# Four chunks to a PSUM bank in the table products of an edge pass, and 320 of 832 pairs by them instead of 416

## The chip, the cores and the metric

One core of a Trainium2 chip runs the whole program. The metric is the device time of one execution in microseconds, shown as the median of three runs; the profile comes from a further execution. A difference under about 0.2% can't be told from none.

## The reference

Four graph layers over the same 200000 edges (`src`, `dst`, sorted by `dst`) and 6250 nodes of 128 features. What the change touches is the edge part of the last layer:

```python
h = jnp.maximum(_layernorm(x, axis=-1), 0.0)
h = jnp.concatenate([h[row], edge_attr], axis=1)
h = jax.nn.relu(h @ W1a + b1a) @ W1b + b1b
sums = jax.ops.segment_sum(h, col, num_segments=n_nodes)
```

The kernel splits the first product: `h @ W1a[:128]` is made once per node (the "table"), `edge_attr @ W1a[128:] + b1a` once per edge (the "edge rows", stored in DRAM as `bucketed`). Per edge it remains to add the table row of its source to its edge row, to take the positive part, and to sum over the edges of each target node; `W1b` comes after the sum. So the rows of the table have to be fetched 200000 times by index.

## The kernel before

Edges are ordered into 49 x 49 = 2401 buckets (target tile of 128 nodes, source tile of 128 nodes), then cut into chunks of 128 edges; two chunks make a pair, and all edges of a pair go to one target tile. There are 832 pairs, 1664 chunks. Two ways lead from an index to a table row:

- **By gather** (the second 416 pairs, `FAR_PAIRS`). GpSimd issues one indirect DMA a chunk (L1841) into `ring`, SyncE loads the pair's edge rows (L1852), VectorE adds them (`message`, L1954), rectifies (`rectify`, L1959), builds the one-hot matrix of the targets (L1947), TensorE multiplies (L1937), VectorE adds the result to the target tile `h` (`add`, L1965). Rings: `ring` and `edge_in` have DEEP = 8 pairs, one-hots four.
- **By products with the table in SBUF** (the first 416 pairs, 832 chunks, `NEAR`). A chunk needs one look-up for each source tile that its edges touch: VectorE compares the chunk's sources, broadcast to all partitions in `rows`, with the numbers of a tile (`looks`, L1979) into one of eight `hot` slots, and TensorE multiplies that one-hot by the table's tile (`look_up`, L1920) and adds it into the chunk's PSUM bank. ScalarE has first copied the chunk's edge rows into that bank (`prepare`, L1873) and afterwards takes the positive part out of it (`evict`, L1880) and stores it to `near_rows` in DRAM, four chunks in one transfer (L1904). A chunk has a whole bank, of which it uses 128 of 512 columns, and there are four banks, 4 to 7.

Which tile and which chunk a look-up belongs to are known only at run time. The lists `chunk_of` and `tile_of` have LOOKS = 3248 entries; TensorE and VectorE each read eight entries of both lists into registers for a pair (L1926, L1928; L1969, L1971) and compute addresses from them. ScalarE reads four ends (L1896): the count of look-ups after which a chunk is whole. LOOKS is the largest count that could occur (832 + 2401 + 2, rounded up); entries behind the real ones point at a dump chunk, number `NEAR`, and are worked off the same way. Waits: a one-hot waits that its chunk's bank is prepared (`s_clear`) and that the look-up seven before it is done (`s_looked`); the look-up waits for the one-hot.

Both ways run side by side in the first block ("block A"). The order on each engine is written out by hand: in pair `n` VectorE does `message(n)`, eight one-hots, `rectify(n)`, `add(n-1)`, the target one-hots of `n+3`; TensorE does eight look-ups and then the product of gathered pair `n`. 416 x 8 places are enough for 3248 entries, so the last ten pairs have no look-ups. The second block ("block B") then reads `near_rows` back in quads of four chunks (L2014, a ring of eight quads) and sums them into the target tiles: one-hots L2036, products L2027, adds L2044.

Of the kernel before, what the change touches and what calls it, by code (L numbers as in the profile page):

```python
# [4 lines left out]
P = 128  # L5
# [51 lines left out]
PER_PAIR = 8  # L57
QUAD = 4
EPS = 1e-5
SLOPE = 0.2  # L60
assert NEAR % (4 * QUAD) == 0 and FAR_PAIRS * PER_PAIR >= LOOKS and LOOKS % PER_PAIR == 0 and MARKS < DUMP
# [55 lines left out]
def build(nc, t, out):  # L117
    ctx = ExitStack()
    with ctx:
# [1021 lines left out]
        def near_tables():  # L1141
# [29 lines left out]
            def vector(e):  # L1171
# [11 lines left out]
                e.scalar_tensor_tensor(chunk_of, low_i.bitcast(i32), float(16 - EARLY), look_no[:, :], ALU.add, ALU.add).then_inc(code.sem, 1)  # L1183
# [3 lines left out]
                e.tensor_scalar(chunk_of.bitcast(i32), chunk_of, float(NEAR + 16), None, op0=ALU.min).then_inc(listed.sem, 1)  # L1187
# [607 lines left out]
        def edge_pass():  # L1795
# [10 lines left out]
            stage = slots(QUAD * P, 2)  # L1806
            tile_of = room(LOOKS).bitcast(i32)[0:1, :]
            chunk_of = part(wide, 0, LOOKS).bitcast(i32)[0:1, :]
            rows = part(wide, LOOKS, 16 * P // 2).bitcast(i16)
            near_edge = part(wide, LOOKS + 16 * P // 2, 3 * QUAD * P).rearrange("p (k w) -> p k w", k=3)  # L1810
            end_of = src_i[0:1, 0:NEAR]
            s_got = [sem(f"meta_got{k}") for k in range(DEEP)]
            s_side = [sem(f"meta_side{k}") for k in range(DEEP)]
# [5 lines left out]
            s_near_edge = [sem(f"near_edge{k}") for k in range(3)]  # L1819
            row_in = [Baton(s_piece[k], 4 * sage_loads) for k in range(4)]  # L1820
# [8 lines left out]
            def bank(c):  # L1829
                return psum[:, 4 + c % 4, 0:P]  # L1830

            with nc.Block() as block:
                @block.gpsimd
                def _(e):
                    for n in range(FAR_PAIRS):
                        k = n % DEEP
                        if n >= DEEP:
                            e.wait_ge(s_pe, n - DEEP + 1)
                        for c in range(PAIR):
                            chunk = (NEAR_PAIRS + n) * PAIR + c  # L1840
                            e.indirect_dma_start(ring[:, k, c, :], None, table,  # L1841
                                                 bass.IndirectOffsetOnAxis(ap=src_i[:, chunk:chunk + 1], axis=0)).then_inc(s_got[k], 16)

                @block.sync
                def _(e):
                    e.dma_start(chunk_of, look_chunk[:, 0:LOOKS]).then_inc(lists.sem, 16)
                    e.dma_start(tile_of, look_tile[:, 0:LOOKS]).then_inc(lists.sem, 16)
                    for n in range(FAR_PAIRS):
                        k = n % DEEP
                        if n >= DEEP:  # L1850
                            e.wait_ge(s_sum, n - DEEP + 1)
                        e.dma_start(edge_in[:, k, :, :], bucketed_v[:, cols(NEAR_PAIRS + n), 0:D]).then_inc(s_side[k], 16)  # L1852

                @block.scalar
                def _(e):
                    def load_edges(g):
                        e.dma_start(near_edge[:, g % 3, :].rearrange("p (c w) -> p c w", c=QUAD),
                                    bucketed_v[:, g * QUAD:(g + 1) * QUAD, 0:D]).then_inc(s_near_edge[g % 3], 16)

                    def load_rows(g):  # L1860
                        at = g % 4 * QUAD * P
                        e.dma_start(rows[:, at:at + QUAD * P], near_src[g * QUAD:(g + 1) * QUAD, :].rearrange("c n -> (c n)").unsqueeze(0)
                                    .broadcast_to([P, QUAD * P])).then_inc(row_in[g % 4].sem, 16)

                    def prepare(c):
                        g = c // QUAD
                        if c == NEAR:
                            e.copy(bank(c), zeros[:, 0:P]).then_inc(s_clear, 1)
                            return
                        if c % QUAD == 0:  # L1870
                            e.wait_ge(s_near_edge[g % 3], 16 * (g // 3) + 16)
                            e.wait_ge(row_in[g % 4].sem, row_in[g % 4].at + 16 * (g // 4) + 16)
                        e.copy(bank(c), near_edge[:, g % 3, c % QUAD * P:(c % QUAD + 1) * P]).then_inc(s_clear, 1)  # L1873

                    def evict(c, end):
                        g = c // QUAD
# [4 lines left out]
                        e.wait_ge(staged.sem, staged.at + c + 1)  # L1881

                    e.sem_inc(s_clear, 15)
                    e.dma_start(end_of, chunk_end[:, 0:NEAR]).then_inc(s_near_out[0], 16)
                    for g in range(3):
                        load_edges(g)
                    for g in range(4):
                        load_rows(g)
                    e.wait_ge(blanked.sem, blanked.at + 4)
                    for c in range(4):  # L1890
                        prepare(c)
                    e.wait_ge(s_clear, 15 + QUAD)
                    load_edges(3)
                    e.wait_ge(s_near_out[0], 16)
                    for g in range(quads):
                        _, end = nc.values_load_multi_w_load_instructions(  # L1896
                            end_of[0:1, g * QUAD:(g + 1) * QUAD], engines=(ENG.Activation,), min_val=1, max_val=LOOKS,
                            skip_runtime_bounds_check_because=reason)
                        for k in range(QUAD):
                            c = g * QUAD + k  # L1900
                            evict(c, end[k])
                            if c + 4 <= NEAR:
                                prepare(c + 4)
                        e.dma_start(near_rows[:, g * QUAD * D:(g + 1) * QUAD * D], stage[:, g % 2, :]).then_inc(s_near_out[g % 2], 16)  # L1904
                        if g + 4 < quads:
                            e.wait_ge(s_clear, 15 + QUAD * (g + 2))
                            load_edges(g + 4)
                            load_rows(g + 4)
# [4 lines left out]
                def _(e):  # L1913
                    for k in range(4):
                        e.matmul(psum[:, 4 + k, 0:P], lhsT=blank[:, 0:P], rhs=blank[:, 0:P], start=True, stop=True).then_inc(blanked.sem, 1)
                    e.wait_ge(lists.sem, lists.at + 32)

                    def look_up(i, chunk, tile):
                        e.wait_ge(look.sem, look.at + i + 1)
                        e.matmul(flat[:, ds((chunk & 3) * 512 + 2048, P)], lhsT=hot[:, i % 8, :], rhs=table_in[:, ds(tile * P, P)],  # L1920
                                 start=False, stop=True, skip_group_check=True).then_inc(s_looked, 1)

                    for n in range(FAR_PAIRS):
                        if n * PER_PAIR < LOOKS:
                            here = slice(n * PER_PAIR, (n + 1) * PER_PAIR)
                            _, chunk = nc.values_load_multi_w_load_instructions(  # L1926
                                chunk_of[0:1, here], engines=(ENG.PE,), min_val=16, max_val=NEAR + 16, skip_runtime_bounds_check_because=reason)
# [178 lines left out]
```

## Time and profile before

| | us |
|---|---|
| median of 3 runs | 9367.44 (9365.83 to 9368.25) |
| the profiled execution | 9366.17 |
| its span | 9364.4 |
| TensorE busy | 7028.5 (75%) |
| VectorE busy | 5660.6 (60%) |
| GpSimd busy | 2656.2 (28%) |
| ScalarE busy | 2515.7 (27%) |
| mean granted clock of TensorE | 0.87 |

Busy time leaves out what an engine's sequencer does by itself: computing addresses, waiting, and reading numbers into registers (TENSOR_LOAD). Such instructions are found under their line, with the engine's name and a q (`PEldq`, `DVEq`). A matmul of float32 leaves two records, so that `x16` in a timeline are eight look-ups. The granted clock is a share of TensorE's full 2.4 GHz; 0.50 is the level of 1.2 GHz.

### The profile page before, as it was taken

What the parts mean: (1) busy time and instruction counts of PE and PEld (TensorE: products, weight loads), DVE (VectorE), ACT (ScalarE), POOL (GpSimd) and SP (SyncE); (2) the same over time, 40 slices, a digit from 0 to 9 for tenths busy, and PEclk for the clock granted to TensorE, in tenths of its full rate; (3) what the DMA queues carried; (4) which work ended last, traced back from release to release, by engine and by line L of the source; (5) the groups of instructions that cost most, each with busy time, mean ns of one, the idle gap of its engine ahead of it and who ended that gap; (6) DMA issues with size and microseconds to landing.
All of it is one profiled execution on the core that took longest, in us unless ns stands there. A gap on an engine that the chain in (4) does not pass through costs nothing. (4 is left out here: it accounts for less than half of the span.)

```text
span 9364.4 us, 133857 instructions
## 1 busy us (share of the span) xinstructions
PE 7028.5 (75%) x35740; PEld 4596.9 (49%) x35792; DVE 5660.6 (60%) x16783; ACT 2515.7 (27%) x5863; POOL 2656.2 (28%) x2952
## 2 busy tenths in 40 slices
PE   4777777775566659940488699999998777777787
PEld 4555555453122224420477544444445666666676
DVE  6777777775589990059899800000014777777786
ACT  0222222222467740020388600000001333310001
POOL 0777777776470000000000000000002444444410
PEclk9767776766679989975799899999999999999998
DMA  3333333334975538849566478787886766642363
GB/s 99 103 103 105 105 104 103 105 105 167 393 231 164 168 114 306 299 195 426 205 215 216 144 262 276 262 287 256 295 284 200 181 180 179 179 111 63 63 178 88
DMA packets 969628, 1759.77 MB, mean 188 GB/s; under 512 B 102288, under 2 KB 665125, under 8 KB 905315
## 3 DMA queue, kind: packets, MB, share of 16 engines
q1 hardware_dynamic: 683820, 1335.73, 44.1%
q0 software_dynamic: 110720, 276.01, 9.0%
q10 hardware_dynamic: 174394, 139.51, 5.5%
q8 instruction: 346, 5.67, 0.3%
q14 instruction: 348, 2.84, 0.1%
HBM read 1412.04 MB, written 338.80 MB: 187 GB/s over the span
## 5 line engine op out<-in xcount | busy, mean ns | idle before, releaser
L768 POOL DMA_INDIRECT bucketed<-arena,wide x1563 | 1515.6, 970 | 726.5 <-issue 714.0
L1920 PE MATMUL psum<-wide,arena 128*128 x6496 | 1209.9, 329 | 400.5 <-DVE arena L1979 393.9
L1920 PEld LDWEIGHTS psum<-wide,arena 128*128 128x128 f32 x6496 | 989.9, 195 | 618.3 <-issue 493.3
L1787 POOL DMA_DIRECT2D table<-wide x13 | 9.7, 743 | 4316.2 <-DVE wide L1711 4316.2
L1979 DVE TENSOR_SCALAR arena<-wide,tile_first 128x128 f32 x3248 | 870.8, 300 | 472.3 <-PE psum L1920 293.8
L1841 POOL DMA_INDIRECT arena<-table,src_i x832 | 803.3, 966 | 1009.1 <-PE psum L1937 872.4
L1660 PE MATMUL psum<-arena,h 128*128 128x512 f32 (+1 forms) x2548 | 1048.6, 570 | 19.1 <-DMA arena<-adjacency 17.5
L922 PE MATMUL psum<-arena 128*128 128x512 bf16 x2253 | 695.7, 442 | 435.0 <-DVE arena L870 259.4
L665 PE MATMUL psum<-arena 128*113 128x177 bf16 x1568 | 534.4, 341 | 416.2 <-ACT wide L687 374.6
L870 DVE TENSOR_SCALAR arena<-sums 128x512 bf16<-128x512 int16 x2304 | 799.9, 347 | 0.0
L659 PE MATMUL psum<-w_edge,arena 128*128 128x256 f32 x1568 | 786.9, 597 | 0.0
L1660 PEld LDWEIGHTS psum<-arena,h 128*128 128x128 f32 x2548 | 470.0, 191 | 573.7 <-issue 552.6
L1546 PE MATMUL psum<-sums,arena 128*128 128x129 f32 x4802 | 602.2, 281 | 154.1 <-DVE arena L1536 154.1
L922 PEld LDWEIGHTS psum<-arena 128*128 128x128 bf16 x2304 | 240.5, 104 | 883.5 <-issue 722.3
L869 DVE TENSOR_SCALAR arena<-sums 128x128 bf16<-128x128 int16 x2304 | 582.7, 253 | 127.5 <-PE psum L922 126.5
L1546 PEld LDWEIGHTS psum<-sums,arena 128*128 128x128 f32 x4802 | 555.8, 192 | 200.6 <-DVE arena L1536 200.5
L687 ACT CAST wide<-psum 49x49 f16<-49x49 f32 x1568 | 311.6, 199 | 973.9 <-PE psum L665 750.7
L665 PEld LDWEIGHTS psum<-arena 128*113 128x113 bf16 x1568 | 262.9, 168 | 624.5 <-ACT wide L687 623.6
L603 PE MATMUL psum<-blank 128*128 128x120 bf16 x3296 | 531.9, 261 | 18.6 <-PEq L101 18.6
L1660 PE MATMUL psum<-arena,sums 128*128 128x512 f32 (+1 forms) x1274 | 524.1, 571 | 9.3 <-DMA arena<-adjacency 8.6
L1220 PE MATMUL psum<-arena,h 128*128 128x512 f32 (+1 forms) x1274 | 518.5, 570 | 8.8 <-DMA arena<-adjacency 8.6
L1734 DVE TENSOR_TENSOR arena<-psum,wide 128x512 f32<-128x512 f32 (+1 forms) x39 | 25.5, 659 | 786.5 <-PE psum L1660 784.2
(398 smaller groups left out, 11006.0 us busy)
## 6 DMA issues: line engine op xcount, KB each, us to landing
arena<-adjacency SPq DMA_DIRECT2D x294, 1024.0 KB
arena<-adjacency SPq DMA_DIRECT2D x98, 1568.0 KB, 7.8
adjacency<-wide SPq DMA_DIRECT2D x588, 256.0 KB
arena<-adjacency SPq DMA_DIRECT2D x196, 640.0 KB, 3.9
arena<-adjacency SPq DMA_DIRECT2D x147, 768.0 KB
arena<-bucketed POOLq DMA_DIRECT2D x208, 528.0 KB, 6.0
arena<-adjacency SPq DMA_DIRECT2D x49, 1792.0 KB, 6.9
arena<-adjacency SPq DMA_DIRECT2D x49, 1344.0 KB, 6.1
```

The lines of the kernel that those rows point to most:

```text
L603: e.matmul(spare, lhsT=blank[:, 0:P], rhs=blank[:, 0:spare.shape[1]], start=first, stop=True, skip_group_check=True)
L659: e.matmul(terms(k, c), lhsT=attr[k][:, at:at + P], rhs=W["edge"][:, :, :].rearrange("p c n -> p (c n)"), start=True, stop=True)
L665: update = e.matmul(psum[0:SPAN, 0, 0:TILES + P], lhsT=hot[k][:, c, by_dst], rhs=hot[k][:, c, by_both], start=False, stop=True, skip_group ...
L768: e.indirect_dma_start(bucketed, bass.IndirectOffsetOnAxis(ap=places[k][0:size, c:c + 1], axis=0), rows[k][0:size, c, :], None).then_inc(s ...
L869: e.tensor_scalar(hot_src[:, k, :], from_one[:, 0:P], row_of[:, ds(i * RUN + k, 1)], None, op0=ALU.is_equal)
L870: e.tensor_scalar(hot_key[:, k, :], from_one[:, 0:GROUP * P], key_of[:, ds(i * RUN + k, 1)], None, op0=ALU.is_equal).then_inc(s_ready, 1)
L922: e.matmul(flat[:, ds((bucket[k] & (BANKS - 1)) * 512, 512)], lhsT=hot_src[:, k, :], rhs=hot_key[:, k, :], start=False, stop=True, skip_gr ...
L1546: last = e.matmul(psum[:, 4 * (r % 2) + c // 3, 129 * (c % 3):129 * (c % 3) + 129], lhsT=slots[n % 4][:, c * P:(c + 1) * P], rhs=node_rhs( ...
L1660: last = e.matmul(psum[:, 4 * (p % 2) + j, 0:width], lhsT=nodes[:, q * P:(q + 1) * P], rhs=pieces[n % 4][:, 512 * j:512 * j + width], star ...
L1841: e.indirect_dma_start(ring[:, k, c, :], None, table, bass.IndirectOffsetOnAxis(ap=src_i[:, chunk:chunk + 1], axis=0)).then_inc(s_got[k], 16)
L1920: e.matmul(flat[:, ds((chunk & 3) * 512 + 2048, P)], lhsT=hot[:, i % 8, :], rhs=table_in[:, ds(tile * P, P)], start=False, stop=True, skip ...
L1979: e.tensor_scalar(hot[:, i % 8, :], rows[:, ds((chunk[k] & 15) * P, P)], tile_first[:, ds(tile[k], 1)], None, op0=ALU.is_equal).then_inc(l ...
```

## The change

- 320 pairs (640 chunks) go by products, 512 pairs by gathers. LOOKS becomes 3048, and six entries are worked off in a pair instead of eight; 508 pairs have look-ups, four have none.
- A bank holds a quad of four chunks. `prepare` copies 512 columns at once and counts four, `evict` takes 512 columns at once when the last of the four is whole. ScalarE reads 16 ends for four quads. The window is four banks of four chunks.
- The one-hot ring has 16 slots instead of 8; `rows` holds 32 chunks instead of 16, loaded eight chunks at a time.
- To make room, `ring` and `edge_in` hold FAR = 4 pairs instead of 8. Block B's ring of quads has four places instead of eight.

```diff
-NEAR_PAIRS = PAIRS // 2
+NEAR_PAIRS = 320
+PER_PAIR = 6
-LOOKS = -(-(NEAR + BUCKETS_49 + 2) // 16) * 16
+LOOKS = -(-(NEAR + BUCKETS_49 + 2) // PER_PAIR) * PER_PAIR
-PER_PAIR = 8
+HOTS = 16
+FAR = 4
+NEAR_BANKS, ROW_QUADS, EDGE_QUADS = 4, 8, 3
+LIST_FROM = ROW_QUADS * QUAD
...
-            ring = slots(PAIR * P, DEEP).rearrange("p k (c w) -> p k c w", c=PAIR)
-            edge_in = slots(PAIR * P, DEEP).rearrange("p k (c w) -> p k c w", c=PAIR)
+            ring = slots(PAIR * P, FAR).rearrange("p k (c w) -> p k c w", c=PAIR)
+            edge_in = slots(PAIR * P, FAR).rearrange("p k (c w) -> p k c w", c=PAIR)
-            hot = slots(P, 8)
+            hot = slots(P, HOTS)
-            def bank(c):
-                return psum[:, 4 + c % 4, 0:P]
+            def bank(q):
+                return psum[:, 4 + q % NEAR_BANKS, :]
...
                     for n in range(FAR_PAIRS):
-                        k = n % DEEP
-                        if n >= DEEP:
-                            e.wait_ge(s_pe, n - DEEP + 1)
+                        k = n % FAR
+                        if n >= FAR:
+                            e.wait_ge(s_pe, n - FAR + 1)
...
-                    def load_rows(g):
-                        at = g % 4 * QUAD * P
+                    def load_rows(r):
+                        n = 2 * QUAD
+                        at = r % (ROW_QUADS // 2) * n * P
...
-                        e.copy(bank(c), near_edge[:, g % 3, c % QUAD * P:(c % QUAD + 1) * P]).then_inc(s_clear, 1)
+                        e.copy(bank(q), near_edge[:, q % EDGE_QUADS, :]).then_inc(s_clear, QUAD)
+                        if q + EDGE_QUADS < quads:
+                            e.wait_ge(s_clear, LIST_FROM - 1 + QUAD * (q + 1))
+                            load_edges(q + EDGE_QUADS)
...
-                        if c % QUAD == 0 and g >= 2:
-                            e.wait_ge(s_near_out[g % 2], 16 * (g // 2) + 16 * (g % 2 == 0))
-                        e.activation(stage[:, g % 2, c % QUAD * P:(c % QUAD + 1) * P], bank(c), ACT.Relu).then_inc(staged.sem, 1)
+                        if q >= 2:
+                            e.wait_ge(s_near_out[q % 2], 16 * (q // 2) + 16 * (q % 2 == 0))
+                        e.activation(stage[:, q % 2, :], bank(q), ACT.Relu).then_inc(staged.sem, 1)
...
-                    for g in range(quads):
-                        _, end = nc.values_load_multi_w_load_instructions(
-                            end_of[0:1, g * QUAD:(g + 1) * QUAD], engines=(ENG.Activation,), min_val=1, max_val=LOOKS,
-                            skip_runtime_bounds_check_because=reason)
-                        for k in range(QUAD):
-                            c = g * QUAD + k
-                            evict(c, end[k])
-                            if c + 4 <= NEAR:
-                                prepare(c + 4)
+                    for q in range(quads):
+                        if q % 4 == 0:
+                            _, end = nc.values_load_multi_w_load_instructions(
+                                end_of[0:1, q * QUAD:(q + 4) * QUAD], engines=(ENG.Activation,), min_val=1, max_val=LOOKS,
+                                skip_runtime_bounds_check_because=reason)
+                        evict(q, end[q % 4 * QUAD + QUAD - 1])
+                        if q + NEAR_BANKS <= quads:
+                            prepare(q + NEAR_BANKS)
...
-                        e.matmul(flat[:, ds((chunk & 3) * 512 + 2048, P)], lhsT=hot[:, i % 8, :], rhs=table_in[:, ds(tile * P, P)],
+                        e.matmul(flat[:, ds((chunk & (NEAR_BANKS * QUAD - 1)) * P + 2048, P)], lhsT=hot[:, i % HOTS, :], rhs=table_in[:, ds(tile * P, P)],
...
-                                if i >= 8:
-                                    e.wait_ge(s_looked, i - 6)
+                                if i >= HOTS:
+                                    e.wait_ge(s_looked, i - HOTS + 2)
...
+            quad_in = FAR
-                        if g >= DEEP:
-                            e.wait_ge(near_pe.sem, near_pe.at + 2 * (g - DEEP) + 2)
+                        if g >= quad_in:
+                            e.wait_ge(near_pe.sem, near_pe.at + 2 * (g - quad_in) + 2)
```

On ScalarE, in block A, before: the work on one quad, between two loads of ends (`near_rows` is the store, `bucketed` the edge rows, `near_src` the sources).

```order
L1896 TENSOR_LOAD src_i
L1880 ACTIVATE arena<-psum 128x128 [waits near_looked]
L1873 COPY psum<-wide 128x128 [waits sage_piece2,near_edge2,sage_lin]
L1880 ACTIVATE arena<-psum 128x128 [waits near_looked]
L1873 COPY psum<-wide 128x128 [waits sage_lin]
L1880 ACTIVATE arena<-psum 128x128 [waits near_looked]
L1873 COPY psum<-wide 128x128 [waits sage_lin]
L1880 ACTIVATE arena<-psum 128x128 [waits near_looked]
L1873 COPY psum<-wide 128x128 [waits sage_lin]
L1904 DMA near_rows<-arena 128x512
L1857 DMA wide<-bucketed 128x4x128 [waits near_clear]
L1862 DMA wide<-near_src 128x512
```

The same place after the change, two quads.

```order
L1887 ACTIVATE arena<-psum 128x512 [waits near_out0,near_looked]
L1878 COPY psum<-arena 128x512 [waits near_edge0,near_rows3,sage_lin]
L1861 DMA arena<-bucketed 128x4x128 [waits near_clear]
L1908 DMA near_rows<-arena 128x512
L1887 ACTIVATE arena<-psum 128x512 [waits near_out1,near_looked]
L1878 COPY psum<-arena 128x512 [waits near_edge1,sage_lin]
L1861 DMA arena<-bucketed 128x4x128 [waits near_clear]
L1908 DMA near_rows<-arena 128x512
L1867 DMA wide<-near_src 128x1024
```

Eight instructions on PSUM for a quad have become two, and the sources come once in two quads. On GpSimd, at the start of block A, the gathers that are issued before the first wait for a product are, before:

```order
L1841 DMA arena<-table,src_i 128x128 x16
L1841 DMA arena<-table,src_i 128x128 [waits meta_pe]
L1841 DMA arena<-table,src_i 128x128
L1841 DMA arena<-table,src_i 128x128 [waits meta_pe]
L1841 DMA arena<-table,src_i 128x128
```

and after the change:

```order
L1845 DMA arena<-table,src_i 128x128 x8
L1845 DMA arena<-table,src_i 128x128 [waits meta_pe]
L1845 DMA arena<-table,src_i 128x128
L1845 DMA arena<-table,src_i 128x128 [waits meta_pe]
L1845 DMA arena<-table,src_i 128x128
```

Eight pairs of gathers ran ahead of the products, now four.

## Rows read from the trace of the kernel before

**Rows 1.** The page: span and instructions, busy time of each engine.
```profile
span 9364.4 us, 133857 instructions
PE 7028.5 (75%) x35740; PEld 4596.9 (49%) x35792; DVE 5660.6 (60%) x16783; ACT 2515.7 (27%) x5863; POOL 2656.2 (28%) x2952
```

**Rows 2.** Windows: us, busy PE, PEld, DVE, ACT, POOL, granted clock, DMA share, GB/s.
```profile
7165.00:7700.00 535.00, 415.28 (x2389) 351.33 (x2388) 386.91 (x1428) 209.25 (x784) 237.33 (x248) 0.96 0.70 181
8300.00:8600.00 300.00, 238.76 (x1415) 200.03 (x1415) 227.89 (x854) 0.00 (x0) 136.32 (x142) 1.00 0.25 65
```

**Rows 3.** Lines L1926 (all, 7170 to 8290, 8300 to 8935), L1896, L915.
```profile
L1926 PEldq TENSOR_LOAD <-wide x406: 587/592/1431, 7149.9 to 8943.5; - x136
...
L1926 PEldq TENSOR_LOAD <-wide x249: 587/592/1431, 7172.1 to 8289.7; - x125
...
L1926 PEldq TENSOR_LOAD <-wide x150: 587/590/606, 8303.4 to 8935.0; - x150
...
L1896 ACTq TENSOR_LOAD <-src_i x208: 307/314/587, 7157.1 to 8293.8; - x104
...
L915 PEldq TENSOR_LOAD <-wide x144: 1102/1567/2637, 2300.2 to 3456.0; - x144
```

**Rows 4.** Timeline of TensorE, 8500 to 8513: start, us, line, idle before.
```profile
8504.36 2.92 PE L1920 MATMUL psum<-wide,arena 128*128 x16 [0.89 <-DVE arena L1979]
8507.11 0.61 PE L1937 MATMUL psum<-arena 128*128 128x128 f32 x4
8508.59 2.90 PE L1920 MATMUL psum<-wide,arena 128*128 x16 [0.86 <-DVE arena L1979]
8511.32 0.61 PE L1937 MATMUL psum<-arena 128*128 128x128 f32 x4
8512.76 0.48 PE L1920 MATMUL psum<-wide,arena 128*128 x2 [0.83 <-DVE arena L1979]
```

**Rows 5.** Timeline of VectorE in the same stretch.
```profile
8505.92 2.21 DVE L1979 TENSOR_SCALAR arena<-wide,tile_first 128x128 f32 x8 [0.98 <-PE psum L1920]
...
8509.83 1.80 DVE L1979 TENSOR_SCALAR arena<-wide,tile_first 128x128 f32 x6 [0.63 <-PE psum L1920]
```

**Rows 6.** Waits from 7170 to 8290: who for whom, us, times, longest.
```profile
DVE arena L1979 <- PE psum L1920: 176.7, 226, 2.5
DVE arena L1979 <- ACT psum L1873: 90.9, 111, 3.6
```

**Rows 7.** Timeline of GpSimd, 8500 to 8513.
```profile
8503.74 0.95 POOL L1841 DMA_INDIRECT arena<-table,src_i  x1 [2.11 <-PE psum L1937]
8504.99 0.94 POOL L1841 DMA_INDIRECT arena<-table,src_i  x1 [0.30 <-issue]
```

**Rows 8.** Groups by line: evictions from 7170 to 8290, a wide copy behind block B.
```profile
L1880 ACT ACTIVATE arena<-psum 128x128 f32<-128x128 f32 x819 | 225.9, 276 | 658.3 <-PE psum L1920 560.2 <-issue 86.9
...
L1074 ACT COPY arena<-psum 128x896 f32<-128x896 f32 x14 | 12.6, 898 | 19.4 <-PE psum L1045 19.4
```

**Rows 9.** Lines L1841 and L2014, and the timeline at the end of block A.
```profile
L1841 POOL DMA_INDIRECT arena<-table,src_i x832: 938/944/7147, 7147.6 to 8955.0; - x167
...
L2014 SPq DMA_DIRECT2D arena<-near_rows x208: 319/320/1005, 8963.4 to 9205.3; - x104
...
8960.62 0.42 DVE L1954 TENSOR_TENSOR arena<-arena 128x256 f32<-128x256 f32 x1 [1.21 <-DMA arena<-table,src_i]
...
8966.14 6.07 PE L2027 MATMUL psum<-arena 128*128 128x128 f32 x30 [3.48 <-DMA arena<-near_rows]
```

**Rows 10.** Groups by line in block B, 8970 to 9210.
```profile
L2044 DVE TENSOR_TENSOR h<-h,psum 128x128 f32 x402 | 111.8, 278 | 2.4 <-issue 1.1 <-PE psum L2027 0.9
```

**Rows 11.** Timeline of TensorE, 7263 to 7273, and the window 7265 to 7271.
```profile
7267.40 3.78 PE L1920 MATMUL psum<-wide,arena 128*128 x16 [0.62 <-DVE arena L1979]
...
7271.66 1.42 PE L1920 MATMUL psum<-wide,arena 128*128 x8
...
7265.00:7271.00 6.00, 5.38 (x25) 5.09 (x25) 4.12 (x16) 1.95 (x8) 1.97 (x2) 0.50 0.68 175
```

More of the change, by code:

```diff
@@ L1800, in slots @@
                 return room(n * k).rearrange("p (k w) -> p k w", k=k)
[L1802 to L1803 removed]
+            ring = slots(PAIR * P, FAR).rearrange("p k (c w) -> p k c w", c=PAIR)
+            edge_in = slots(PAIR * P, FAR).rearrange("p k (c w) -> p k c w", c=PAIR)
             onehot = slots(PAIR * P, 4).rearrange("p k (c w) -> p k c w", c=PAIR)
[L1805 removed]
+            hot = slots(P, HOTS)
             stage = slots(QUAD * P, 2)
+            near_edge = slots(QUAD * P, EDGE_QUADS)
             tile_of = room(LOOKS).bitcast(i32)[0:1, :]
             chunk_of = part(wide, 0, LOOKS).bitcast(i32)[0:1, :]
[L1809 to L1810 removed]
+            rows = part(wide, LOOKS, ROW_QUADS * QUAD * P // 2).bitcast(i16)
             end_of = src_i[0:1, 0:NEAR]
[L1812 to L1813 removed]
+            s_got = [sem(f"meta_got{k}") for k in range(FAR)]
+            s_side = [sem(f"meta_side{k}") for k in range(FAR)]
             s_hot, s_sum, s_msg, s_pe, s_add = (sem("meta_" + n) for n in ("hot", "sum", "msg", "pe", "add"))
@@ L1818, in edge_pass @@
             s_clear, s_looked = sem("near_clear"), sem("near_looked")
-            s_near_edge = [sem(f"near_edge{k}") for k in range(3)]
-            row_in = [Baton(s_piece[k], 4 * sage_loads) for k in range(4)]
+            s_near_edge = [sem(f"near_edge{k}") for k in range(EDGE_QUADS)]
+            s_near_rows = [sem(f"near_rows{k}") for k in range(ROW_QUADS // 2)]
             s_near_out = [sem(f"near_out{k}") for k in range(2)]
@@ L1884, in _ @@
-                    e.dma_start(end_of, chunk_end[:, 0:NEAR]).then_inc(s_near_out[0], 16)
[L1885 to L1893, printed above, removed]
-                    e.wait_ge(s_near_out[0], 16)
@@ new lines, in _ @@
+                    for q in range(EDGE_QUADS):
+                        load_edges(q)
+                    for r in range(ROW_QUADS // 2):
+                        load_rows(r)
+                    e.wait_ge(blanked.sem, blanked.at + NEAR_BANKS)
+                    for q in range(NEAR_BANKS):
+                        prepare(q)
+                    e.wait_ge(s_near_out[0], 16)
+                    for q in range(quads):
[6 more added lines that the diff above has]
+                            prepare(q + NEAR_BANKS)
+                        e.dma_start(near_rows[:, q * QUAD * D:(q + 1) * QUAD * D], stage[:, q % 2, :]).then_inc(s_near_out[q % 2], 16)
+                        if q % 2 == 1 and q // 2 + ROW_QUADS // 2 < quads // 2:
+                            load_rows(q // 2 + ROW_QUADS // 2)
@@ L1913, in _ @@
                 def _(e):
-                    for k in range(4):
-                        e.matmul(psum[:, 4 + k, 0:P], lhsT=blank[:, 0:P], rhs=blank[:, 0:P], start=True, stop=True).then_inc(blanked.sem, 1)
+                    for k in range(NEAR_BANKS):
+                        e.matmul(psum[:, 4 + k, :], lhsT=blank[:, 0:P], rhs=blank[:, :], start=True, stop=True).then_inc(blanked.sem, 1)
                     e.wait_ge(lists.sem, lists.at + 32)
@@ L1936, in _ @@
                         for c in range(PAIR):
-                            last = e.matmul(psum[:, n % 4, 0:D], lhsT=onehot[:, n % 4, c, :], rhs=ring[:, n % DEEP, c, :], start=c == 0, stop=c == PAIR - 1)
+                            last = e.matmul(psum[:, n % 4, 0:D], lhsT=onehot[:, n % 4, c, :], rhs=ring[:, n % FAR, c, :], start=c == 0, stop=c == PAIR - 1)
                         last.then_inc(s_pe, 1)
@@ L1976, in looks @@
                                 e.wait_ge(s_clear, chunk[k + 1])
-                                if i >= 8:
-                                    e.wait_ge(s_looked, i - 6)
-                            e.tensor_scalar(hot[:, i % 8, :], rows[:, ds((chunk[k] & 15) * P, P)], tile_first[:, ds(tile[k], 1)], None,
+                                if i >= HOTS:
+                                    e.wait_ge(s_looked, i - HOTS + 2)
+                            e.tensor_scalar(hot[:, i % HOTS, :], rows[:, ds((chunk[k] & (ROW_QUADS * QUAD - 1)) * P, P)], tile_first[:, ds(tile[k], 1)], None,
                                             op0=ALU.is_equal).then_inc(look.sem, 1)
```

72 lines of the change are left out of this document (33 added, 39 removed).

## The prediction

> **What bounds the kernel now.** I read the page's totals first [rows 1]: TensorE is the busiest engine with 75% of the span, but this is an average over a dozen stages. The change touches one stage, so I cut that stage into stretches [rows 2]. The edge pass has two blocks. Block A (look-ups beside gathers) runs from the first load of L1926 at 7149.9 [rows 3] to the first load of block B at 8963.4 [rows 9], 1813.5 us; block B (sums of the stored rows) goes on to about 9214. The rest, 7147 us before and some 150 us behind, is almost untouched.
>
> Block A has two parts. A pair (eight look-ups, two gathered chunks) takes (8289.7 - 7172.1)/248 = 4.51 us while ScalarE works, and (8935.0 - 8303.4)/149 = 4.24 us later, when ScalarE is idle [rows 2, 3]. Why a second part: LOOKS is an upper bound, the 832 chunks reach only half of the 2401 buckets, some 832 + 1200 = 2032 real look-ups, 254 pairs. The other 1216 entries point at the dump chunk and cost the same two engine instructions.
>
> What fills 4.24 us when nobody waits for ScalarE? The timeline of TensorE [rows 4] shows it: from the first look-up of a pair (8504.36) to its gathered product (8507.11) 2.75 us, 0.344 a look-up; then 1.48 us until the next pair's first look-up (8508.59), of which the product itself is 0.61. The pair after it is the quickest shown: 2.73 us for eight (0.341) and 1.44 us, 4.17 together. The hole is the sequencer: two TENSOR_LOADs a pair (chunk and tile numbers) at 0.59 us each stand between the product and the next look-up [rows 3]. They are not counted as busy, so in the page this time looks like idle. VectorE has the same shape [rows 5]: 2.21 us for eight one-hots, the rest other operations and its own two loads, 3.91 us from first one-hot to first one-hot when it isn't held up. So the pair is bound by two sequencers of nearly equal period, TensorE's a little longer, and the waits between them [rows 6] are mostly the shorter one waiting for the longer. GpSimd needs 1.25 us for a gather [rows 7], 2.5 us a pair, and waits for TensorE the rest.
>
> **The change part by part.**
> 1. *More pairs by gathers, with six entries each.* 508 pairs with look-ups instead of 406 (3048/6, 3248/8), and 4 instead of 10 bare ones. This multiplies the constant part of a pair by 1.25; 200 look-ups fewer save little (200 x 0.341 = 68 us).
> 2. *The loads become shorter.* A load of 6 numbers occurs nowhere in the trace. Nearest: 4 numbers 0.314 us on ScalarE, 8 numbers 0.59 us on TensorE, 16 numbers 1.10 us at its shortest [rows 3]. Each number costs about 0.07 us; 6 give 0.45. Bounds: 0.314 and 0.59. I take 0.45, it lies on the line; two loads save 0.27 us a pair. The Trainium skill ("DMA: Bandwidth & Descriptors", latency and other measured facts) gives tensor_load a floor of about 600 ns. ScalarE's 0.314 us speaks against it; by that floor nothing would be saved.
> 3. *Pair without waits for ScalarE:* TensorE, by its quickest pair, 6 x 0.341 + 1.44 - 0.27 = 3.22 us (by the mean of 4.24 it would be 3.29). VectorE, whose loads I take to be as long: 3.91 - 2 x 0.276 - 0.27 = 3.09, and a load of eight tile numbers every eighth pair adds 0.08, 3.17. TensorE stays the longer by a hair. Sixteen one-hot slots instead of eight take away the wait of a one-hot for the look-up seven before it, so that each engine may be a pair ahead.
> 4. *Four chunks a bank.* ScalarE now does one eviction and one preparation of 512 columns where it did four of 128. 128 columns take 0.276 us, 896 take 0.898 [rows 8]; on that line 512 take about 0.58. So 1.2 us for four chunks instead of 2.2, and the DMA issues as before, the one for the sources halved. ScalarE wasn't the bound, it waited 0.56 ms for look-ups; what counts is the window: 16 chunks (about 39 real look-ups, 6.5 pairs) instead of 4. The 91 us in which one-hots waited for a preparation go [rows 6]. They are part of 4.51 - 4.24 = 0.27 us a pair. The other part is slower loads: with ScalarE's transfers about, L1926 reaches 1.43 us, without them 0.606 at most [rows 3]. This stays, as the same bytes a microsecond still move. I keep 0.20 us of the 0.27; the bounds are 0 and 0.27.
> 5. *Real and dump pairs after.* 640 chunks + 2401 x 320/832 = 923 is 1563 real look-ups, 261 pairs at 3.42; 246 further intervals at 3.22. 892.6 + 792.1 = 1684.7 us. The start stays: of the 1793.6 us between the first and the last L1926 [rows 3], 253 intervals of 4.51 and 152 of 4.24 leave 8 us. The end, 8943.5 to 8963.4 [rows 3, 9], 19.9 us, was one full pair and ten bare ones; now one and four, about 10 us. Block A: 1684.7 + 8 + 10 = 1702.7 us, 110.8 less.
> 6. *Gather ring of four pairs instead of eight.* A gather of pair n+4 is issued when product n is done, and needed three pairs later, 9.7 us. The bound on a landing: the last gather is issued at 8955.0 and the last message sum runs at 8960.62 [rows 9], 5.6 us at most; with 1.25 us for the first of the two gathers 6.9 us. Covered, cost 0, the cover is 2.8 us. Edge rows (SyncE) have a ring of four too, with one short transfer a pair: 0.
> 7. *Block B.* 402 pairs in 240 us [rows 10], 0.597 a pair; 96 fewer save 57.3 us. Its ring has four quads instead of eight: from issue (8963.4) to first product (8966.14) 2.8 us [rows 9]; with the quad's own products, 1.1 us, 3.9 us for a turn of four quads that now last 4 x 1.19. Hidden with 0.9 us to spare; I give it 3 us (bounds 0 and 15).
> 8. *The rest* (marks, scans, transposes of fewer blocks, a wider blank product at the start) is a few instructions of some us under long streams: 0.
>
> Sum: -110.8 - 54.3 = -165.1. The profiled execution took 9366.17 us, so 9201; the median of the runs is 1.3 us above it. **Forecast 9202 us.**
>
> The clock isn't a term: at the low level of 1.2 GHz a pair of eight look-ups took 7271.66 - 7267.40 = 4.26 us [rows 11], below the mean 4.51.
>
> **The rivals.**
> - *The loads don't shrink.* The mechanism: a load costs 0.59 us up to eight numbers, so a pair is 6 x 0.341 + 1.44 = 3.49 on TensorE. For: the only TensorE rows are 8 and 16 numbers. Against: these two already differ, and ScalarE's 4. 507 x 0.27 = 137 us more, 9339. Chance 0.09. This is what the floor of the Trainium skill (same page and section) would do here.
> - *The two sequencers don't overlap.* VectorE's 3.17 and TensorE's 3.22 depend on each other at two places in each pair: the product waits for the rectified messages, the one-hot and the add of a pair wait for the product before. If each waits for the other in turn, as in the mean of 4.24 against the quickest pair's 4.17 but more, 0.2 us a pair: 101 us more, 9303. Chance 0.12.
> - *The ring of gathers becomes the bound*, the one that ends slower. Place: L1845, wait for product n-4. A turn is the two gathers (1.25 + landing), then message 0.42, loads 0.9, one-hots 1.7, rectify (no longer than the message) 0.4 and product 0.6: 5.3 us + landing. It decides from 4 x 3.32 = 13.3 us on, a landing of 8 us, and makes the kernel slower than before from 9.5 us on. At 10 us: 15.3/4 = 3.83 us a pair, 507 x 0.51 = 259 us more, 9461. For: half as many in flight, 40% more gathers in a microsecond beside transfers that already take 0.70 of the DMA engines [rows 2]. Against: 5.6 us at most in [rows 9]. Chance 0.04.
> - *The wait for ScalarE was the whole 0.27, and more:* pairs of 3.22 throughout, with a load nearer to 0.4: 9125 to 9150. Inside my main case.
>
> **How the numbers follow.** Main case 0.75 with 9202: its bounds are no extra in the real part (-52), loads shorter by 0.025 us (-25), against no relief at all for the pitch and the extra (507 x 0.07 + 261 x 0.07 = 54) and block B (+12): 9125 to 9268. The range is carried up to the second rival: 9125 to 9310; beyond it lie the first and third. A change under 0.2%, 19 us, can't be told from none here. Faster: 0.94 (all but the third rival and some unnamed failure); same 0.02; slower 0.04.
>
> **What would show it.** Right: block A about 1700 us, interval of TensorE's first load 3.4 us, later 3.2; that load at 0.45 us; almost no one-hot waiting for L1878; a sum waiting for gathers nowhere; block B 0.60 us a pair. Wrong: loads at 0.59 (first rival); both TensorE waiting for VectorE and VectorE for TensorE over 0.3 us a pair (second); VectorE's sum waiting for the gather's landing (third).

## The result, and the profile after

| | before | after |
|---|---|---|
| median | 9367.85 us | 9920.35 us (9914.08 to 9925.58) |
| ratio | | 1.0585, 95% interval 1.0572 to 1.0599 |
| profiled execution | 9366.17 | 9925.58 |
| block A | 1813.5 | 2426.6 (7155.7 to 9582.3) |

The changed kernel is 5.9% slower; 9125 to 9310 us was forecast, with 0.94 for faster. Of the 559 us between the two profiled executions block A brings +613; block A also starts 6 us later, and everything behind it is 60 us shorter (block B alone 59). The page after:

```profile
span 9923.6 us, 130930 instructions
PE 7255.2 (73%) x35337; PEld 4843.7 (49%) x35390; DVE 5663.0 (57%) x16775; ACT 2263.6 (23%) x4519; POOL 2850.9 (29%) x3144
```

Two stretches of block A (us, busy PE, PEld, DVE, ACT, POOL, granted clock, DMA share, GB/s), against [rows 2]:

```profile
7165.00:7700.00 535.00, 370.41 (x1775) 330.77 (x1776) 300.44 (x1108) 80.69 (x137) 214.22 (x224) 0.73 0.52 140
8300.00:8900.00 600.00, 417.69 (x2043) 368.79 (x2043) 348.58 (x1280) 16.04 (x27) 244.15 (x256) 0.75 0.27 69
```

VectorE is busy 56% of the first stretch (it was 72%), and the granted clock is 0.73 and 0.75, where it was 0.96 and 1.00. Both engines wait more, and the question is for what. The lines below are TensorE's first load of a pair (all of them; while ScalarE works; later) and its second load, to be compared with [rows 3]:

```profile
L1928 PEldq TENSOR_LOAD <-wide x508: 818/1352/2199, 7155.7 to 9567.3; - x170
...
L1928 PEldq TENSOR_LOAD <-wide x266: 818/1352/2199, 7174.0 to 8449.1; - x133
...
L1928 PEldq TENSOR_LOAD <-wide x224: 818/1155/1504, 8519.6 to 9557.8; - x112
...
L1930 PEldq TENSOR_LOAD <-arena x508: 820/1475/2262, 7156.6 to 9568.8; - x170
```

A pair takes (8449.1 - 7174.0)/265 = 4.81 us and later (9557.8 - 8519.6)/223 = 4.66 us, forecast 3.42 and 3.22. And a load of six numbers takes 0.82 us at least and 1.35 or 1.48 in the median, where eight took 0.59. The timeline of TensorE, against [rows 4]:

```profile
8601.55 2.74 PE L1922 MATMUL psum<-wide,arena 128*128 x12 [2.68 <-DVE arena L1981]
8604.08 1.06 PE L1939 MATMUL psum<-arena 128*128 128x128 f32 x4
8605.58 2.20 PE L1922 MATMUL psum<-wide,arena 128*128 x12 [0.43 <-issue]
8607.61 0.61 PE L1939 MATMUL psum<-arena 128*128 128x128 f32 x4
8610.83 2.53 PE L1922 MATMUL psum<-wide,arena 128*128 x12 [2.61 <-DVE arena L1981]
```

From product to next look-up there are 1.50 us one time and 3.22 us the next, by turns. In the single loads the pattern is strict: in the later stretch the loads of even pairs take 0.82 us on both engines, those of odd pairs 1.48 us on TensorE and 1.41 on VectorE, in both lists, and no load of an odd pair is as short as one of an even pair. An even pair begins 48 x n/2 bytes into its list, an odd pair 24 bytes further. TensorE's two loads of the odd pair in this timeline, one line each:

```profile
L1928 PEldq TENSOR_LOAD <-wide x1: 1476/1476/1476, 8607.4 to 8607.4; - x1
L1930 PEldq TENSOR_LOAD <-arena x1: 1489/1489/1489, 8609.0 to 8609.0; - x1
```

Waits of the whole edge pass, against [rows 6, 9]:

```profile
PE psum L1922 <- DVE arena L1981: 675.4, 401, 11.9
DVE arena L1981 <- PE psum L1922: 660.0, 405, 3.3
...
PEld psum L2030 <- DMA arena<-near_rows: 24.9, 41, 3.8
...
DVE arena L1956 <- DMA arena<-table,src_i: 6.3, 3, 3.2
```

By the profile TensorE and VectorE wait for each other, 0.68 and 0.66 ms. Most of this is the waiting engine's own reading: the 2.61 us before 8610.83 are put down to VectorE, and the two loads above, which end at 8610.46, cover 2.2 us of them. Laid over the single loads, 503 of the 675 us and 513 of the 660 us are covered by the two loads of the waiting engine itself. VectorE waited for gathers 6.3 us.

### The profile page after: what moved, and what is told of

Its sections match the earlier page's. It is cut to its first block and busy times, and to the rows that moved or that the text cites. A ratio compares the mean times of both kernels' runs of the same rounds, so it can differ in the third digit from the quotient of the medians.

```text
span 9923.6 us, 130930 instructions
## 1 busy us (share of the span) xinstructions
PE 7255.2 (73%) x35337; PEld 4843.7 (49%) x35390; DVE 5663.0 (57%) x16775; ACT 2263.6 (23%) x4519; POOL 2850.9 (29%) x3144
## 3 DMA queue, kind: packets, MB, share of 16 engines
q14 instruction: 333, 2.73, 0.1%
## 5 line engine op out<-in xcount | busy, mean ns | idle before, releaser
L1922 PE MATMUL psum<-wide,arena 128*128 x6096 | 1324.1, 382 | 745.2 <-DVE arena L1981 675.4
L1922 PEld LDWEIGHTS psum<-wide,arena 128*128 128x128 f32 x6096 | 1129.9, 259 | 934.5 <-issue 876.9
L1845 POOL DMA_INDIRECT arena<-table,src_i x1024 | 988.1, 965 | 1438.9 <-PE psum L1939 1275.2
L1981 DVE TENSOR_SCALAR arena<-wide,tile_first 128x128 f32 x3048 | 814.8, 298 | 989.0 <-PE psum L1922 660.0
L952 ACT COPY wide<-psum 128x512 f32<-128x512 f32 x637 | 371.0, 582 | 475.7 <-PE psum L926 299.7
```

The source lines that it names most:

```text
L1845: e.indirect_dma_start(ring[:, k, c, :], None, table, bass.IndirectOffsetOnAxis(ap=src_i[:, chunk:chunk + 1], axis=0)).then_inc(s_got[k], 16)
L1922: e.matmul(flat[:, ds((chunk & (NEAR_BANKS * QUAD - 1)) * P + 2048, P)], lhsT=hot[:, i % HOTS, :], rhs=table_in[:, ds(tile * P, P)], start ...
L1981: e.tensor_scalar(hot[:, i % HOTS, :], rows[:, ds((chunk[k] & (ROW_QUADS * QUAD - 1)) * P, P)], tile_first[:, ds(tile[k], 1)], None, op0=A ...
```

## The experiments

Theory A: a load of numbers is made of accesses, four words each where it starts on a multiple of four words, one word each elsewhere or in the remainder. Rivals: B, only the count matters; C, what ran beside the loads made them slow; D, the loads are a symptom and the ring of four gathers (or the clock) carries the loss. Two of the three chips used took 10250 us for the kernel before instead of 9367; there the first stage takes longer (the last L768 starts at 3124 us in e3_shift4, 2256 in the kernel before), while block A does not (from its first to its last load 1804 us in e3_shift4, 1794 in the kernel before). So each run stands against the kernel before on its own chip, and pairs are compared by their intervals. Runs without a ratio are single executions.

**e1_probe.** A block that reads numbers and uses none:

```diff
+    [nc.values_load_multi_w_load_instructions(words[0:1, 0:6], engines=(ENG.PE,), ...) for _ in range(4)]
```

> The kernel before, and behind the edge pass a block in which TensorE and VectorE each read 1 to 16 numbers into registers from one row of SBUF, four times for each of 16 cases, starting at word 0, 1, 2, 3 or 4 of a 16-word line; nothing uses the numbers. Theory A (a load is made of accesses of about 0.25 us, each of four words where the load starts on a multiple of four words, else of one word): four words at 0: 0.31 us, six at 0: 0.82, six at 2 or 3: 1.47, eight at 0: 0.59, eight at 4: 0.59, eight at 1 or 2: 1.96, twelve at 0: 0.82, sixteen at 0: 1.10. Theory B (only the count matters, multiples of four being quick): six 0.82 to 1.47 at any start, eight 0.59 at any start. Theory C (loads were slow in the changed kernel because of what ran beside them): six at 0 about 0.45. Time of the kernel: 9367 plus 60 to 120 us.

The trace holds none of these loads, whose numbers nothing uses; the run is a repetition of the kernel before (10248.79 against 10256.26) and tells nothing. In e9_probe2 each number read is used.

**e2_shift2, e3_shift4.** The kernel before, its lists moved.

```diff
-            tile_of = room(LOOKS).bitcast(i32)[0:1, :]
-            chunk_of = part(wide, 0, LOOKS).bitcast(i32)[0:1, :]
+            SHIFT_BY = 2
+            tile_of = room(LOOKS + SHIFT_BY).bitcast(i32)[0:1, SHIFT_BY:]
+            chunk_of = part(wide, 0, LOOKS + SHIFT_BY).bitcast(i32)[0:1, SHIFT_BY:]
...
```

> The kernel before, its two lists of numbers moved by two words in SBUF, so that each load of eight starts two words off a multiple of four. Theory A (start of the load): 0.04 + 8 x 0.24 = 1.96 us a load instead of 0.59, 2.74 us more in each of 406 pairs, 9367 + 1112 = about 10480 us. Theory B (count only) and C (what runs beside): 9367 us.

> The same, moved by four words. Theory A with lines of four words: 9367 us, loads of 0.59 us. If the lines that matter are eight words long, the loads would be slower and the kernel up to 10480 us.

What lies behind the lists (`rows`, `near_edge`) moves by as much. In e3_shift4 `SHIFT_BY` is 4.

Moved by two words: 11467.74 against 10256.26, +1211 us, in one execution. Its loads from 10000 to 11000:

```profile
L1927 PEldq TENSOR_LOAD <-wide x144: 1930/1933/1937, 10004.4 to 10994.1; - x144
```

Eight numbers take 1.93 us, the pair 6.92. Moved by four words: 10246.43 us, and

```profile
L1927 PEldq TENSOR_LOAD <-wide x406: 587/592/1425, 8020.2 to 9824.1; - x136
```

Theory A gave 1.96 us and +1112; B and C fall as the whole cause, since the count is the same and so is all that runs beside. That `rows` moved too is no rival: a one-hot takes 0.30 us in both kernels, ScalarE's copy 0.27, and only the loads changed.

**e7_slots_six, e6_slots_eight.** The changed kernel with eight words of list for a pair. The diff is that of e6_slots_eight; e7_slots_six reads `slice(n * SLOT, n * SLOT + PER_PAIR)`.

```diff
-            tile_of = room(LOOKS).bitcast(i32)[0:1, :]
+            SLOT = 8
+            LISTED = LOOKS // PER_PAIR * SLOT
+            tile_of = part(wide, 0, LISTED).bitcast(i32)[32:33, :]
...
-                            here = slice(n * PER_PAIR, (n + 1) * PER_PAIR)
+                            here = slice(n * SLOT, n * SLOT + SLOT)
```

> As slots_eight, but a load reads six numbers, always from a multiple of eight words. Theory A: 0.04 + 3 accesses of 0.26 = 0.82 us each time, none of 1.48; 0.46 us a pair more than slots_eight, so about 235 us more than that kernel, 330 us less than the changed one. Theory B (count only): as slow as the changed kernel.

> The changed kernel with its lists stored with eight words for each pair, of which six are used; a load reads all eight. (Tile numbers on partition 32.) Theory A: loads of 0.59 us, pair of 3.5 us, 1.12 us less than in the changed kernel: 9920 - 570 = 9350 us on the chip of the first result, the same as before within 1%. Theory B (a count of six is slow, eight is quick): the same. Rival D: above 9700 us there.

Six from a start on a multiple of four words ("aligned"), in the stretch without ScalarE:

```profile
L1930 PEldq TENSOR_LOAD <-wide x240: 813/824/841, 9102.0 to 10058.5; - x120
```

None of 1.48 is left, and six are still dearer than eight, so the count matters beside the start. Pair 4.00 us, kernel 10430.83 against 10253 in one execution, 204 us above e6_slots_eight (235 expected). e6_slots_eight reads two numbers that nobody needs:

```profile
L1930 PEldq TENSOR_LOAD <-wide x240: 587/591/608, 9002.8 to 9848.7; - x120
```

Pair 3.54 us, kernel 10227.02, ratio 0.9964 (0.9943 to 0.9985). Everything else of the change is in there, the ring of four too: rival D falls for the loss, and the change without its slow loads is worth 0.4%. The clock follows the loads; granted in the stretch without ScalarE (windows, row shown for e6_slots_eight) it is 1.00 with loads of 0.59 us, 0.85 with 0.82, 0.75 in the changed kernel, 0.68 in e2_shift2 with 1.93.

```profile
9000.00:9850.00 850.00, 643.02 (x3841) 535.81 (x3840) 646.72 (x2402) 0.00 (x0) 462.17 (x481) 1.00 0.33 76
```

**e5_banks_only.** The change without its new split and count.

```diff
-NEAR_PAIRS = 320
+NEAR_PAIRS = 416
-PER_PAIR = 6
+PER_PAIR = 8
...
```

> The changed kernel with the old split and count: 416 pairs by products and 416 by gathers, eight entries a pair; four chunks a bank, the window of 16 chunks, 16 one-hot slots and rings of four stay. (The list of tile numbers lies on partition 32 beside the other one, for room.) Loads are eight numbers on a multiple of four words. Theory A: they take 0.59 us; what is gained is the wait for the preparation and for one-hot slots: 253 pairs at 4.25 to 4.45 instead of 4.51, 152 at 4.17 to 4.24: 20 to 80 us less than the kernel before. Rival D (rings of four carry the loss): slower than before by over 200 us.

10233.86 us, ratio 0.9961 (0.9940 to 0.9983), 19 us less than the kernel before where 20 to 80 were expected. With ScalarE and without:

```profile
L1928 PEldq TENSOR_LOAD <-wide x243: 587/591/1084, 8062.9 to 9118.6; - x122
...
L1928 PEldq TENSOR_LOAD <-wide x137: 587/589/594, 9200.5 to 9776.8; - x137
```

(9118.6 - 8062.9)/242 = 4.36 us and 4.24 us: banks, window and one-hot slots together take away 0.15 us of 4.51 where ScalarE works and nothing elsewhere. They weren't tried one by one.

**e4_two_pairs, e8_ring8.** Twelve numbers every second pair; then also rings of eight.

```diff
-                            here = slice(n * PER_PAIR, (n + 1) * PER_PAIR)
+                            if n % 2 == 0:
+                                here = slice(n * PER_PAIR, (n + 2) * PER_PAIR)
...
-FAR = 4
+FAR = 8
...
```

> The changed kernel, but TensorE and VectorE read twelve numbers of each list every second pair instead of six in each pair. Twelve numbers start on a multiple of four words each time. Theory A: 0.82 us a load, so 0.82 us of loads a pair instead of 2.30; pair about 3.2 us, granted clock of block A near 1.0 again, kernel 9920 - 508 x 1.4 to 1.5 = 9160 to 9210 us. Rival D (the gather ring of four pairs, or the fall of the clock for another reason, carries the loss): above 9600 us. Rival B (count, twelve as slow a number as six): 9700 us or more.

> The kernel that reads twelve numbers every second pair, with rings of eight pairs (gathers, edge rows) and eight quads instead of four. (Tile numbers on partition 32.) In its timeline two pairs come 2.5 us apart and then one gap of 4.2 us, and the gathers of two pairs take 5.0 us. If the ring of four holds the pairs at 3.4 and 3.55 us instead of 3.22: 50 to 120 us less than with four. If it is the two sequencers or the clock: within 20 us of it, of which the waits for near_rows in block B are up to 25 us.

10147.19 us, ratio 0.9894 (0.9855 to 0.9933), and 10162.01, 0.9898 (0.9866 to 0.9930): the ring changes nothing beyond the spread. Both gain 1.1% or 1.0%, where theory A expected 1.7 to 2.2% of e4_two_pairs (9160 to 9210 us). Loads of e8_ring8, an interval being two pairs:

```profile
L1929 PEldq TENSOR_LOAD <-wide x122: 844/851/1501, 8064.5 to 8927.2; - x122
...
L1929 PEldq TENSOR_LOAD <-wide x112: 843/848/857, 9034.9 to 9788.0; - x112
```

3.56 and 3.39 us a pair, not the 3.2 of theory A. Two pairs follow at once and then both engines read twice in a row; look-ups in e8_ring8:

```profile
9304.21 2.32 PE L1922 MATMUL psum<-wide,arena 128*128 x12 [1.86 <-DVE arena L1989]
...
9307.05 2.19 PE L1922 MATMUL psum<-wide,arena 128*128 x12
...
9311.06 2.33 PE L1922 MATMUL psum<-wide,arena 128*128 x12 [1.37 <-DVE arena L1989]
```

From product to product there are 2.61 and 4.18 us by turns, in the mean of the later stretch.

**e10_stagger.** e8_ring8 with the two lists read at different pairs. TensorE's part of the diff, against e8_ring8:

```diff
-            chunk_of = part(wide, 0, LOOKS).bitcast(i32)[0:1, :]
+            chunk_of = part(wide, 2, LOOKS).bitcast(i32)[0:1, :]
...
-                            if n % 2 == 0:
-                                here = slice(n * PER_PAIR, (n + 2) * PER_PAIR)
+                            if n == 0 or n % 2 == 1:
+                                here = slice(n * PER_PAIR, min((n + (2 if n else 1)) * PER_PAIR, LOOKS))
                                 _, chunk = ...
+                            if n % 2 == 0:
+                                here = slice(n * PER_PAIR, (n + 2) * PER_PAIR)
                                 _, tile = ...
...
```

> As ring8 (twelve numbers at a time, rings of eight), but the loads of a pair of pairs are parted: tile numbers at even pairs, chunk numbers at odd pairs (the list of chunks moved by two words so that each load still starts on a multiple of four). The same number of loads, 0.85 us in each pair instead of 1.70 in every second. If the lumps make the two engines wait for each other at 3.40 and 3.55 us a pair: pairs of 3.2 to 3.3 us, 50 to 100 us less than ring8, 150 to 190 less than the kernel before. If the loads cost the same wherever they stand: within 20 us of ring8.

9153.43 us against 9367.14, ratio 0.9772 (0.9758 to 0.9785): faster than both kernels, by 214 us against the one before, where 150 to 190 were expected. Its chunk loads (an interval is two pairs), its timeline, and its windows as above:

```profile
L1929 PEldq TENSOR_LOAD <-wide x139: 843/850/1667, 7167.6 to 8077.8; - x139
...
L1929 PEldq TENSOR_LOAD <-wide x110: 843/849/862, 8103.0 to 8787.5; - x110
```

```profile
8502.93 2.20 PE L1922 MATMUL psum<-wide,arena 128*128 x12 [0.47 <-DVE arena L1993]
8504.96 0.61 PE L1943 MATMUL psum<-arena 128*128 128x128 f32 x4
8506.01 2.17 PE L1922 MATMUL psum<-wide,arena 128*128 x12 [0.44 <-DVE arena L1993]
```

```profile
7165.00:7700.00 535.00, 433.02 (x2586) 365.81 (x2584) 436.81 (x1613) 118.73 (x200) 316.80 (x329) 0.98 0.74 204
8300.00:8600.00 300.00, 254.18 (x1531) 213.51 (x1530) 258.50 (x957) 0.00 (x0) 185.12 (x191) 1.00 0.33 85
```

3.30 us a pair, later 3.14; the gap from product to look-up is 1.05 us and the clock 0.98 and 1.00. The same loads cost 0.25 us a pair more when they come in lumps. Why isn't parted: the engines stand still together, and the granted clock was 0.94 in e8_ring8's later stretch.

**e9_probe2.** VectorE reads and uses numbers of one row. Each line is one count and start:

```diff
+                        _, v = nc.values_load_multi_w_load_instructions(tile_i[0:1, 2:10], engines=(ENG.DVE,), ...)
+                        e.tensor_copy(part(wide, j, 1), tile_first[:, ds(v[-1], 1)])
```

> The kernel before, and behind the edge pass VectorE alone reads 1 to 16 numbers of one row into registers, three times for each of 16 pairs of count and starting word, each read followed by a copy that uses the last number. Theory A (accesses of four words from a start on a multiple of four, else single words; 0.26 us for four words, 0.24 for one, 0.04 fixed): 1 word 0.3; 2 words 0.55; 3 words 0.8; 4 at 0: 0.31; 4 at 1 or 2: 1.0; 6 at 0: 0.82; 6 at 2: 1.47; 7 at 0: 1.1; 8 at 0 or 4: 0.59; 8 at 1 or 2: 1.9; 12 at 0: 0.85; 12 at 2: 2.9; 16 at 0: 1.1. If only two starts in three are slow, or three words cost less than four, the theory's form is wrong though its numbers for six and eight hold.

The lines below are, in order, numbers at start word: 1 at 0, 3 at 0, 4 at 0, 4 at 1, 6 at 0, 6 at 2, 8 at 0, 8 at 2, 8 at 4, 12 at 0, 12 at 2, 16 at 0.

```profile
L2066 DVEq TENSOR_LOAD <-tile_i x3: 303/304/313, 9210.5 to 9211.4; - x3
L2072 DVEq TENSOR_LOAD <-tile_i x3: 744/745/745, 9213.9 to 9215.7; - x3
L2075 DVEq TENSOR_LOAD <-tile_i x3: 344/351/353, 9216.6 to 9217.6; - x3
L2078 DVEq TENSOR_LOAD <-tile_i x3: 957/958/976, 9218.1 to 9220.3; - x3
L2084 DVEq TENSOR_LOAD <-tile_i x3: 811/827/830, 9224.7 to 9226.7; - x3
L2087 DVEq TENSOR_LOAD <-tile_i x3: 1398/1410/1416, 9227.6 to 9230.8; - x3
L2093 DVEq TENSOR_LOAD <-tile_i x3: 596/601/605, 9235.9 to 9237.4; - x3
L2099 DVEq TENSOR_LOAD <-tile_i x3: 1839/1844/1844, 9244.1 to 9248.1; - x3
L2102 DVEq TENSOR_LOAD <-tile_i x3: 592/599/605, 9250.1 to 9252.0; - x3
L2105 DVEq TENSOR_LOAD <-tile_i x3: 843/844/844, 9252.7 to 9254.7; - x3
L2108 DVEq TENSOR_LOAD <-tile_i x3: 2718/2731/2734, 9255.7 to 9261.5; - x3
L2111 DVEq TENSOR_LOAD <-tile_i x3: 1098/1104/1105, 9264.3 to 9266.8; - x3
```

Three words (0.745) cost twice as much as four (0.35). From word 0, one, two and three words take 0.30, 0.525 and 0.745 us, 0.22 for each further word; 4, 8, 12 and 16 take 0.35, 0.60, 0.84 and 1.10, 0.25 for each further four. From word 2 each word costs 0.22 again, twelve take 2.73. That is theory A's form; its figures were near (2.9 expected for twelve from word 2, the largest miss). Eight from word 4 are as quick as from word 0, so what matters is a multiple of four words, not of eight.

**e11_changed.** The changed kernel on the chip of e10_stagger.

> The changed kernel itself beside the others on this chip. Theory A: about 550 us above the kernel before, 575 above slots_eight, 375 above slots_six, loads of 0.82 and 1.48 us by turns.

9924.45 against 9367.14, 1.0595 (1.0579 to 1.0612): e10_stagger is 771 us below it, with the same work on the data. Whether the kernel before would gain from reading its lists in the same way wasn't tried.

## Why the prediction was wrong

*Step 2 failed. No other term was off by more than some 25 us.* It priced a load of six by a straight line between four and eight, 0.45 us, with 0.59 as the upper bound, in "the loads become shorter". Six cost 0.82 where the start is a multiple of four words and 1.48 where it isn't, 1.15 in the mean. For two loads a pair that is 2.30 instead of 0.90: 1.40 us x 508 = 711 us, and 9202 + 711 = 9913, against 9920 measured. That it is so near is in part luck: step 3 was 0.05 us a pair too low, 25 us, and step 4 kept 0.05 us too much, 13 us. The bounds were wrong too: all the rows that I had put beside it, 4, 8 and 16 numbers, are multiples of four from aligned starts, so the line through them said nothing about six. The chances of the main case and the three rivals add up to 1.00, and in none of them does a load take more than 0.59 us, so nothing was left for what came. A better row was in the trace of before. L940 on ScalarE reads 13 numbers at starts of 13 x q words, one in four of them aligned:

```profile
L940 ACTq TENSOR_LOAD <-wide x49: 1000/3137/3693, 2269.9 to 3392.2; - x49
```

Every fourth of these 49 loads takes 1.0 to 1.6 us, the others 2.8 to 3.7, for fewer numbers than the 16 that take 1.10 on TensorE [rows 3]. I did not look at it. Nor does the rule of the Trainium skill ("DMA: Bandwidth & Descriptors", latency and other measured facts), a floor of about 600 ns for tensor_load, hold here: four aligned numbers take 0.35 us on VectorE, one number 0.30.

*Step 1 and 3, the form, held.* A pair of six look-ups without its two loads is 6 x 0.341 + 1.44 - 1.18 = 2.31 us, one of eight 2.99. Adding the measured loads gives what the kernels' intervals show when ScalarE is idle, except where the loads come in lumps:

| kernel | loads a pair | sum | measured | granted clock |
|---|---|---|---|---|
| e10_stagger | 0.85 | 3.16 | 3.14 | 1.00 |
| e6_slots_eight | 1.18 | 3.49 | 3.54 | 1.00 |
| e7_slots_six | 1.64 | 3.95 | 4.00 | 0.85 |
| changed | 2.30 | 4.61 | 4.66 | 0.75 |
| before, eight look-ups | 1.18 | 4.17 | 4.24 | 1.00 |
| e2_shift2, eight look-ups | 3.86 | 6.85 | 6.92 | 0.68 |
| e8_ring8, in lumps | 0.85 | 3.16 | 3.39 | 0.94 |

My first rival (loads of 0.59, 3.49 us a pair) is e6_slots_eight. Its kernel came out level with before (0.9964), as 9339 said (0.9970).

*Step 4, the banks:* I kept 0.20 of the 0.27 us; 0.12 (e5_banks_only) to 0.16 (e10_stagger) stay. One eviction takes 0.60 us for 0.58 expected. The sign that I had named, almost no one-hot waiting for L1878, did not show in the changed kernel. These are the waits of its block A and, below, of e5_banks_only from 8050 to 9150:

```profile
DVE arena L1981 <- ACT psum L1878: 91.3, 44, 2.9
...
DVE arena L1981 <- ACT psum L1878: 7.2, 9, 1.4
```

The first is as much as the 90.9 us of [rows 6], but about four fifths of it are covered by VectorE's own loads. With eight numbers a load the wait is gone, so the window did what step 4 said.

*Step 5:* the last eviction of the changed kernel starts at 8415.7, (8415.7 - 7155.7)/4.81 = 262 pairs after the start; 261 were counted.

```profile
L1887 ACT ACTIVATE arena<-psum x160: 597/598/600, 7174.3 to 8415.7; 128x512 f32<-128x512 f32 x160
```

*Step 6, the ring of four:* right, gathers landed in time and e8_ring8 gained nothing. The rate of gathers was to rise by a third, though (4.4 to 3.3 us a pair), not by the 40% that I wrote. Landing of the gathers in the changed kernel, and block B's loads:

```profile
DMA to landing us min/median/max: 2.4/2.6/5.4
...
L2017 SPq DMA_DIRECT2D arena<-near_rows x160: 319/320/1327, 9582.3 to 9769.5; - x160
```

*Step 7:* (9769.5 - 9582.3)/159 = 1.177 us a quad; before 1.169, with [rows 9], so about 1 us for 3 expected. Block B became 59 us shorter, 54 were expected. *Step 8* was 0, and block A started 6 us later.

*The second rival* (the engines don't overlap) was to be known by both engines waiting for each other over 0.3 us a pair. In the changed kernel they do, 675.4/508 = 1.33 and 660.0/508 = 1.30 us. But this sign could tell nothing: it was met before the change. There VectorE's 176.7 us [rows 6] are 0.71 us in each of 249 pairs, and TensorE's in the same stretch are 0.99:

```profile
PE psum L1920 <- DVE arena L1979: 246.3, 241, 2.1
```

So it isn't mostly the shorter engine that waits for the longer, as I had read; the loads lie in both waits. Where this rival's 0.2 us do occur is in e4_two_pairs and e8_ring8, 0.25 us a pair with loads in lumps.

*The clock* wasn't a term and became an effect: with two loads in each pair it fell further the longer they were. No cost of its own shows in these pairs: they lie within 0.07 us of the sum, and no further off at 0.68 than at 1.00. The timeline after the change shows where the slower look-ups go. From 8601.5 to 8604.1 the granted clock is 0.64, and the six look-ups take 2.53 us to the product instead of 2.03; but the gap behind them is 1.50 us, where 3.22 - 2 x 0.66 = 1.90 would be left with two short loads for two long ones. The sequencer began to read at 8603.45, 0.63 us before the product, and so the reading ran beside the look-ups. The clock was not tried apart from the loads.

## What to carry to other kernels

Price an instruction that the trace doesn't show by rows that share its awkward property (a start, a remainder, a stride), not only its size; if all neighbours are aligned and the new one isn't, there is no upper bound yet. When numbers steer a kernel, read them in multiples of four words from multiples of four words, pad or read too much rather than too little, and spread the reads over the rounds. Such reads don't count as busy, and the profile can put their time down to the other engine: look for them wherever all engines seem to wait for one another. And before a sign is named for a rival, see whether the kernel before already shows it.

## What the runs showed of the hardware

A TENSOR_LOAD of eight numbers takes 0.59 us on TensorE and 0.60 on VectorE from word 0 or 4, and 1.93 and 1.84 us from word 2 (e2_shift2, e9_probe2); two words of shift made a whole kernel 1211 us slower. Fewer numbers can take longer (three 0.745, four 0.35; six from word 0 0.83, eight 0.60). In this loop of two engines, reading two lists in a row every second pair cost 0.25 us a pair more than reading one list in each (3.39 against 3.14 us).
